# An expert layer's step on TensorE: the results' products of the last step moved behind the second up product

## What is computed

```python
shared_out = jnp.einsum('tsh,shd->td', jax.nn.silu(sg) * su, sw2)
rw, sel = jax.lax.top_k(logits, K)                       # K = 2 of E = 8 experts
cw = (jax.nn.one_hot(sel, E, dtype=x.dtype) * rw[..., None]).sum(axis=1)
g = jnp.einsum('td,edh->teh', xf, w1)
u = jnp.einsum('td,edh->teh', xf, w3)
eo = jax.nn.silu(g) * u
moe_out = jnp.einsum('te,teh,ehd->td', cw, eo, w2)
```

## Time and profile before

| | before |
|---|---|
| median of 3 runs | 1832.92 us (1830.34 to 1835.52) |
| profiled execution | 1831.43 us |
| its span | 1829.7 us |
| mean granted TensorE clock | 0.979 |
| expert part | from about 915 us to the end |
| one routed step of full width | 17.6 us |

### The profile page before, as it was taken

The page is one execution under the profiler, slowest core; times in us unless marked ns, Lnnn a source line. Parts: engine busy times, 40 slices in busy tenths (PEclk is TensorE's granted clock), DMA queues, the critical chain, the costliest instruction groups (busy, mean ns, idle before and its releaser), DMA issues.

```text
span 1829.7 us, 35717 instructions
## 1 busy us (share of the span) xinstructions
PE 1704.1 (93%) x12058; PEld 1285.0 (70%) x12058; DVE 1260.7 (69%) x3090; ACT 1094.5 (60%) x2075; POOL 1180.1 (64%) x1438
## 2 busy tenths in 40 slices
PE   3789899998999899999789999999999999999998
PEld 2545555555555555554378888888888889988887
DVE  6789888888888988877635445545445545476666
ACT  5346676766666576766646666666666667433332
POOL 4465567776677687755447777777777778474443
PEclk9879999999999999999889999999999999999999
DMA  2344444454445554546565666666657676465443
GB/s 90 128 140 131 128 144 150 156 165 142 153 147 169 152 162 151 159 158 206 176 213 188 205 221 195 221 201 221 209 192 235 195 233 209 136 197 187 149 150 98
DMA packets 246902, 313.81 MB, mean 172 GB/s; under 512 B 31562, under 2 KB 211412, under 8 KB 240596
## 3 DMA queue, kind: packets, MB, share of 16 engines
q1 hardware_dynamic: 234452, 278.13, 47.9%
q0 software_dynamic: 12288, 33.57, 5.7%
HBM read 211.70 MB, written 99.39 MB: 170 GB/s over the span
## 4 chain that ended last, share of the span: by engine, by line
PE 47%; ACT 1%; DMA 1%; POOL 1%; DVE 1%; issue 0%; SPq 0%; DVEq 0%; ACTq 0%
PE gu L2177 29%; PE yp L2191 15%; PE xt L2166 2%; DMA early_raw<-layernorm_rows 0%; DMA early_raw<-in_L_ffn_w_dram 0%; DVE hf L2047 0%; ACT hid_h L1950 0%; ACT sil L1948 0%; POOL even_up_l L1847 0%; POOL even_dn_l L1847 0%; POOL w_up_l L1847 0%; POOL rows L1909 0%; ACT even_up_h L1942 0%; SPq L1735 0%; DVE xc L2058 0%
## 5 line engine op out<-in xcount | busy, mean ns | idle before, releaser
L705 ACT ACTIVATE pT<-st_ps 128x512 f32<-128x512 f32 x682 | 368.4, 562 | 260.8 <-PE st_ps L1457 252.4
L1033 DVE CUSTOM_DVE_ANT_0 s_ps<-s_ps,masks 128x384 f32<-128x384 f32 (+1 forms) x512 | 314.8, 632 | 42.4 <-PE s_ps L1436 37.5
L2047 DVE TENSOR_TENSOR hf<-sil,gu 128x512 f32<-128x512 f32 (+1 forms) x216 | 140.8, 652 | 262.0 <-ACT sil L1948 262.0
L1436 PE MATMUL s_ps<-k_aug,q_aug 97*128 97x512 bf16 (+3 forms) x1024 | 262.0, 309 | 28.3 <-DVE mx L1033 20.0
L1455 PE MATMUL st_ps<-q_aug,k_aug 99*128 99x512 bf16 (+1 forms) x992 | 269.6, 304 | 10.2 <-ACT pT L705 6.0
L2050 DVE TENSOR_TENSOR hid_l<-hf,hid_h 128x512 fp32r<-128x512 f32 (+1 forms) x216 | 171.6, 795 | 144.8 <-ACT hid_h L1950 144.8
L1950 ACT ACTIVATE hid_h<-hf 128x512 fp32r<-128x512 f32 (+1 forms) x216 | 130.6, 604 | 176.7 <-DVE hf L2047 176.7
L1948 ACT ACTIVATE sil<-gu 128x512 f32<-128x512 f32 (+1 forms) x216 | 121.5, 563 | 166.3 <-PE gu L2177 166.3
L1855 POOL DMA_INDIRECT got<-expert_results,place x128 | 125.3, 979 | 130.9 <-DVE hf L2047 103.3
L1457 PE MATMUL st_ps<-masks,identb 128*128 128x128 bf16 x992 | 194.8, 222 | 0.0
L2177 PE MATMUL gu<-xc,w_up_h 128*128 128x512 f32 (+1 forms) x640 | 182.8, 371 | 2.8 <-POOL w_up_l L1847 2.7
(11 more groups left out here) (303 smaller groups left out, 4506.4 us busy)
## 6 DMA issues: line engine op xcount, KB each, us to landing
w_raw<-in_L_ffn_w_dram SPq DMA_DIRECT2D x60, 512.0 KB, 6.5
early_raw<-in_L_ffn_w_dram SPq DMA_DIRECT2D x57, 512.0 KB
part_scr<-parts SPq DMA_DIRECT2D x64, 384.0 KB, 4.1
q_aug<-part_scr SPq DMA_DIRECT2D x192, 128.0 KB
k_aug<-part_scr SPq DMA_DIRECT2D x192, 128.0 KB
early_raw<-expert_rows SPq DMA_DIRECT2D x34, 512.0 KB, 4.0
expert_results<-yo SPq DMA_DIRECT2D x32, 512.0 KB, 3.3
x_sb<-in_L_attn_x_dram SPq DMA_DIRECT2D x16, 512.0 KB, 4.2
```

Of the source, the lines that this page charges most:

```text
L705: fn(pT[j][:, h:h + heads], unit_view(column_bank(b, u), heads, w), ACT.Exp).then_inc(exp_done, 1)
L1033: vec.tensor_tensor_reduce(bank[:, 0:keys], bank[:, 0:keys], masks[:, 2 * C + P - keys:2 * C + P], 1.0, LOWEST, ALU.add, ALU.max, mx[:, h ...
L1436: last = mm(v[:, n], q_aug[par][0:ROWS_S, h0 + n, P * q:P * (q + 1)], k_aug[par][0:ROWS_S, h0 + n, 0:keys], start=heads == 1, stop=n == he ...
L2047: vec.tensor_tensor(hf[:, m % 2, 0:w], sil[:, m % 2, 0:w], gu[m % 2][:, 1, 0:w], ALU.mult).then_inc(h_done, 1)
```

## The change

In every routed step the down product of the last step is issued behind up product 1, where it was behind up product 0 and the transposes. Nothing else is changed; no engine but TensorE has another order.

```diff
@@ -2202,10 +2202,11 @@
                 pe.wait_ge(xl_done, NC * (n + 1))
                 up(n, 0, par, wpar)
                 transposes(n + 1)
+                up(n, 1, par, wpar)
                 if not known(n) or n:
                     pe.wait_ge(w_low, PIECES * n)
                     down(n - 1, 1 - par, SHARED if known(n) and n == 1 else 1 - par)
-                for m in range(1, NH):
+                for m in range(2, NH):
                     up(n, m, par, wpar)
```

## The result

| | before | after |
|---|---|---|
| median | 1831.63 us (1829.71 to 1835.52, 4 runs) | 1868.56 us (1867.51 to 1869.20, 4 runs) |
| ratio | | 1.0199, 95% interval 1.0183 to 1.0215 |
| profiled execution, span | 1831.43, 1829.7 us | 1867.51, 1865.8 us |
| step 1's transposes to step 32's | 546.0 us | 576.4 us |
| step 32's to step 39's | 79.5 us | 84.7 us |

A forecast was written before the change was run, and what follows sets the result against it. TensorE was taken to bound the kernel, nearly without idle time. Terms of 31.0 + 0.6 + 4.0 + 1.0 = 36.6 us on the profiled 1831.4 gave 1868.0, a median of 1869.5 us; range 1858 to 1874, widened to 1856 to 1882.

The forecast's parts named there:

- main term: Whole-width steps 2 to 32: about 1.0 us of new TensorE idle time in each, 31 us.
- What bounds: Expert part: TensorE alone sets the end, 17.6 us per whole-width step; any late operand's delay is added to the end.
- The chain of 6.45 us: Down product's end through copy, tile 1, cut and low halves to the next step: 6.45 us, against TensorE ready at 5.49.
- Full-width steps, 31.6 us: Steps 1 to 32: 31 x 1.0 us for steps 2 to 32, plus 0.6 us for step 1.
- Half-width steps, 5.0 us: Steps 33 to 39: 4.0 us lost in steps 35 to 38, 0.5 us each in 33 and 34, 0 in 39.
- The other waits hold; the squares are over in time: Whole-width steps: tiles 2 and 3 come in time; even steps' norm squares end before the copy, so the same 1.0 us follows.
- Late weights cost nothing: Odd steps' transfers land 1.5 us late for ScalarE's cut, costed at nothing; rival with loads 3 us longer: 1889 us, 6%.
- The clock stays: TensorE's granted clock stays at 1.00 despite about 1 us idle in every step.
- the rival: Half clock for one up product after each of some 35 stalls: 95 us more, 1964 us; 3%.
- What the new profile would show: Low-half waits some 31 times, about 31 us; ScalarE's copy in the chain; TensorE busy time unchanged; clock 1.00; steps 18.55 us.
- The base: Kernel before: profiled execution 1831.4 us, 1.5 us under the runs' median of 1832.9, from which the forecast median was set.

The follow-up runs named there:

- e5: The changed kernel, but SP asks for the weights of step n + 2 first in full-width steps too; 1869.04 us, ratio 1.0189.
- e1: The changed kernel, but in full-width steps ScalarE cuts weight pieces 2 and 3 ahead of the result's copy; 1843.32 us, ratio 1.0057.
- e2: The changed kernel, but in full-width steps ScalarE copies the result behind tile 1 and the cut of pieces 2 and 3; 1845.24 us, ratio 1.0063.
- e6: e2, and in half-width steps ScalarE does tile 1 ahead of its wait for the down product; 1843.15 us, ratio 1.0059.
- e10: e1 with SP asking for the weights of step n + 2 first in full-width steps too; 1840.51 us, ratio 1.0043.
- e9: e6 with SP asking for the weights of step n + 2 first in full-width steps too; 1829.75 us, ratio 0.9983.
- e8: The changed kernel with the down product behind up product 2 as well, leaving one up product behind it; 1978.62 us, ratio 1.0797.
- e12: The kernel before, with ScalarE's cut of weight pieces 2 and 3 ahead of the result's copy; 1829.89 us, ratio 0.9988.

## Why the prediction was right

The mechanism and the size of its main term were right. That the total meets the forecast within 1 us is in part luck: several small terms missed in opposite directions, and the step-by-step loss adds up to 35.7 us, not 36.9.

- *What bounds.* TensorE packed without gaps, an end that moves with every late operand: held. The stalls of the 31 full-width steps, 30.4 us, went to the end one for one. That no wait showed at a step's start was true of the matmuls only; the weight loads waited 0.20 us.
- *The chain of 6.45 us.* Measured 6.37, each link within 0.03 but for the last (0.05 instead of 0.11). The first three matmuls after a stall take 0.12 more than undisturbed ones, which I did not have (0.06 of it was there in the kernel before). The sum of 1.0 us per step is met because the two errors cancel.
- *Full-width steps, 31.6 us.* Measured 30.4 from step 1's to step 32's transposes (step 1: 0.5, predicted 0.6) and 0.6 more behind step 32: 31.0.
- *Half-width steps, 5.0 us.* Steps 35 to 38 lost 4.3 (predicted 4.0); of steps 33 and 34 the first lost 0.4 and the second nothing (0.5 each).
- *The other waits hold; the squares are over in time.* Held: odd and even steps are alike at 18.57 to 18.66.
- *Late weights cost nothing.* Held for this change, by e5. For e1, e2 and e6 I costed the same term at nothing again without a new walk; it was worth 3 us in e1 (e10) and 13 in e6 (e9).
- *The clock stays.* Held: the granted clock is 1.00 with a stall of 1.0 us in every step. The rule of the Trainium skill that I set against the row (TensorE: Matmul & The Clock Gate, "A second HAM failure mode: psum-queue depth-cycling") says that frequent short idle pieces between groups of matmuls make TensorE's clock go back and forth between its two levels. The trace of the changed kernel does not agree with it. In e8, with 2.4 us in each step, the trace agrees, though the clock's share there was some 9 us and not the 95 of the rival.
- *What the new profile would show.* The releasers of the waits, the step lengths and the clock came as said. The waits add up to 26.3 us instead of 31, since the view counts from the modelled end of a matmul, and TensorE's busy time rose from 1704.1 to 1712.1 us instead of staying. The chain of waits did not come as said: it names GpSimd's list instead of ScalarE's copy.
- *The base.* The forecast stood on a median before of 1832.9; the result's own runs gave 1831.6. The changed trace also lost 0.9 us ahead of step 1's transposes and won 0.4 behind the last step's, neither of which is the change's work as far as is known.

## What to carry to other kernels

Moving work ahead of a product takes cover away from whatever stands behind that product. Before such a move, walk the chain from the product's end to the next thing that the bound engine waits for, in each other engine's own order, and compare it with what is left to hide it; a wait that the profile does not show may be one with zero slack. If the move is wanted, the other engines' lists and the load queue must move with it (e9). Here giving slack to the operand alone did as much (e12), and either gain was only 0.1%.

## What the runs showed of the hardware

- Stalls of 1.0 us in every step left the granted clock at 1.00. A stall of 2.4 us in every step (e8) brought the mean to 0.94 to 0.96: in about two steps of three an up product ran mostly at half clock behind the stall and took some 4.4 us instead of 2.74. In the kernel before a single stall of 2.75 us had no such effect, so the length of one stall does not decide alone.
- After a stall the first three up matmuls take 0.80 us from start to start. They take 0.74 where the first weight load had to wait 0.20 us for its operand, and 0.68 where it waited for nothing.
- VectorE's subtraction hid_l (both inputs in SBUF) takes 0.69 us by itself. Begun while a GpSimd operation ran, it took up to 1.85 us (e10) and 2.95 us (e8), and all those of 1.0 us or more in both traces ended 0.54 to 0.56 us behind the end of the GpSimd operation. VectorE's product hf, with one input in PSUM, kept 0.67 to 0.69 us.
